# A gated attention and expert kernel: input rounding moved into the first steps, output projection one step later

## The chip, the cores and the metric

The kernel runs on one core of one Trainium2 chip. A core has five engines, each with its own queue of instructions: TensorE (PE in the profile), VectorE (DVE), ScalarE (ACT), GpSimd (POOL) and SyncE (SP, which here only issues transfers). They wait for each other by semaphores. The metric is the time of one execution on the device in microseconds, and the median over several runs.

## What is computed

```python
x = x + tanh(g_xattn) * xattn(layernorm(x), ctx)      # 4 batches of 256 tokens, 256 channels
x = x + tanh(g_ffn) * moe(layernorm(x))               # 64 experts, 6 for each token, 64 slots each
# xattn: h = ln(layernorm(x)); 8 groups of 2 heads, 128 channels a head
q, k, v = (fp8(bf16(clip(h / s_in))) * s_in @ W.T * w_scale for self attention)
qx      = the same with its own scale and weights; kx, vx = ctx @ w_kv_x.T   # cross attention
q, k, qx, kx = ln(each head)
out = concat(softmax(q k' / sqrt(128)) v, softmax(qx kx' / sqrt(128)) vx)    # 4096 channels
out = fp8(bf16(clip(out / smooth))) @ wproj.T * scale
```

`fp8(...)` is a rounding to 8-bit floats (4 exponent, 3 mantissa bits). All the rest is in 32 bits: matrix products take each operand as a high and a low part where it isn't exact.

## The kernel before

**Prologue (0 to some 60 us).** SP loads x by batch, then small vectors, the context, weights and eight scalars. DVE normalises each batch twice (`ln_step`), TensorE transposes (`transpose_h`), ScalarE applies the weights (`ln_out`) and divides by the four input scales (`quant_y`, eight activations a batch). `quant(b)` on DVE clips and rounds with four linked operations (clip, mask of the exponent, scale of the mask, addition), and `quant_sub(b)` on GpSimd subtracts into `xq`, the rounded rows. All four batches are done there, with two sets of scratch memory for them (`q_y`, `q_mg`). Key and value weights are transposed and split (`fill_kv`, `kv_hi`, `kv_lo`), then query weights.

**Attention loop.** There are 32 sub-heads: a = (group pair j, batch b, group in the pair). Step i of 34 (`NSUB + MAXLAG`) works on three of them: `s0 = sub(i)` is projected (`project_q`), normalised (`squares_q` on ACT, `sums` on DVE, `rstd_q` on GpSimd, `scaled_q` on DVE) and transposed (`fill_Tq`, `fill_Tk`; the high and low parts by `q_hi` and `qk_lo`); `s1 = sub(i-1)` has its four rows of `scores`, `maxes`, `exps`, `recip`, `p_norm` (GpSimd), transposes of the probabilities (`fill_pT`, `evac_pT`) and products with the values (`fill_pv`); `s2 = sub(i-2)` is rounded (`y_of`, `magic`, `round_cat`) and goes through the output projection `fill_op`, whose sum `add_acc` adds to `acc`. One half of the keys and values of a later batch is projected in every step (`project_kv`). Each engine's list is written out by hand in the order of execution.

**Buffers.** `proj_ps` holds one projection at a time. Two banks `aux_ps` alternate over all fills in the order that `all_fills` lists, so each fill waits until the one two places ahead is evacuated. `weight_fills(i, slot)` says which new weights are transposed in which step, by position `i % 8`.

**End.** In steps 32 and 33 `x1_stats(b)` adds the attention's result to x and takes the statistics for batch b, `f_pow(b)` (GpSimd) and `x1_norm(b)` (DVE) normalise, `fill_fT` transposes and `router_logits` scores the experts. Then the experts are chosen, rows gathered and 32 pairs of experts computed.

The profile's line numbers of the main parts: 509 `quant_sub`, 526 `rstd_of`, 541 `p_norm`, 548 and 551 `round_cat`, 665 `quant_y`, 792 `exps`, 806 `y_of`, 978 `weight_scales`, 987 to 990 `quant`, 1014 `kv_lo`, 1083 `scaled_q`, 1097 `maxes`, 1117 `magic`, 1143 to 1153 `x1_stats`, 1457 `project_q`, 1471 `fill_Tq`, 1501 `scores`, 1534 `fill_op`.

## Time and profile before

| | us |
|---|---|
| median of 3 runs (lowest, highest) | 824.04 (821.97, 824.12) |
| the profiled execution | 820.62 |
| its span, from the first to the last instruction | 818.80 |
| TensorE busy in the span | 724.2 (88%) |
| VectorE busy | 607.0 (74%) |
| ScalarE busy | 464.3 (57%) |
| GpSimd busy | 455.8 (56%) |

The span has some 60 us of prologue, about 570 of attention steps, 50 of tail and router, and 137 of experts. Busy shares say how full an engine is, not which one sets the pace: that is read from the waits in each stage. A duration in a timeline is that of a group of like instructions, and the time in square brackets is how long the engine stood idle before it and what ended this.

### The profile page before, as it was taken

Reading aid. Unit: us, or ns where it says so; the run is one execution under the profiler, and the core shown is the slowest. Engines: PE = TensorE matmul, PEld = TensorE weight load, DVE = VectorE, ACT = ScalarE, POOL = GpSimd, SP = SyncE. Lnnn points to the kernel's source line nnn. Section 1 sums busy time; section 2 is a strip of 40 time slices with the busy share of each in tenths; the row PEclk is TensorE's granted clock in tenths of the full one; section 3 lists DMA queues with packets and bytes.
Section 4 is the critical chain, followed back from the end, with each engine's and each line's share of the span. In section 5 each row is a group of like instructions: output and inputs, shape, how many; then the busy total and the mean of one; then the engine's idle time right before and its main releaser. Section 6 shows DMA issues by size and latency. Waiting matters only on the chain.

```text
span 818.8 us, 15329 instructions
## 1 busy us (share of the span) xinstructions
PE 724.2 (88%) x4859; PEld 586.4 (72%) x4859; DVE 607.0 (74%) x1290; ACT 464.3 (57%) x1178; POOL 455.8 (56%) x592
## 2 busy tenths in 40 slices
PE   3548999899999989999998999999976786999996
PEld 2536877788878777887877887887754554777775
DVE  6856888787888878888887888887887692444554
ACT  3646767667676766767666776766743231222221
POOL 3464767666667756676765667676655313222220
PEclk9869999999999999999999999999999796999999
DMA  5310000100000010000001010000020103666661
GB/s 181 107 54 26 1 27 1 49 30 27 27 1 27 1 53 26 26 27 2 27 1 52 2 33 27 1 2 0 1 59 1 38 28 109 192 186 189 198 193 53
DMA packets 44479, 42.74 MB, mean 52 GB/s; under 512 B 3718, under 2 KB 43387, under 8 KB 44411
## 3 DMA queue, kind: packets, MB, share of 16 engines
q1 hardware_dynamic: 42874, 36.62, 14.8%
q0 software_dynamic: 1536, 5.28, 2.4%
q8 instruction: 35, 0.57, 0.3%
q14 instruction: 34, 0.27, 0.1%
HBM read 39.52 MB, written 2.37 MB: 51 GB/s over the span
## 4 chain that ended last, share of the span: by engine, by line
PE 50%; DVE 19%; ACT 12%; issue 9%; POOL 7%; SPq 2%; DMA 1%; DVEq 0%; ACTq 0%; POOLq 0%
PE out_ps L1717 8%; PE aux_ps L1534 8%; PE proj_ps L1442 5%; ACT p_sb L792 5%; DVE q_tok L1083 4%; PE aux_ps L1471 4%; PE pT_ps L1510 4%; PE proj_ps L1433 4%; PE work_ps L1709 3%; POOL y_bf L548 3%; POOL catq L551 3%; PE work_ps L1731 2%; PE s_ps L1501 2%; ACT y_bf L806 2%; PE proj_ps L1457 2%
## 5 line engine op out<-in xcount | busy, mean ns | idle before, releaser
L541 POOL TENSOR_SCALAR p_sb<-p_sb,psum_row 128x256 f32<-128x256 f32 x256 | 121.1, 488 | 78.9 <-DVE psum_row L1102 78.8
L792 ACT ACTIVATE p_sb<-s_ps,negmax 128x256 f32<-128x256 f32 x256 | 118.0, 474 | 33.5 <-DVE negmax L1097 32.7
L1108 DVE COPY pT_sb<-pT_ps 128x512 f32<-128x512 f32 x128 | 87.7, 686 | 52.0 <-PE pT_ps L1510 50.9
L1520 PE MATMUL aux_ps<-pT_sb,v_sb 128*128 128x512 f32 x256 | 121.2, 595 | 3.5 <-DVE pT_sb L1108 3.5
L548 POOL TENSOR_TENSOR y_bf<-y_bf,mg_bf 128x512 bf16<-128x512 bf16 x64 | 86.1, 1345 | 63.8 <-DVE mg_bf L1120 63.8
L1501 PE MATMUL s_ps<-kT,qT 128*128 128x256 f32 x768 | 115.1, 292 | 6.0 <-DVE qT L1093 3.8
L1501 PEld LDWEIGHTS s_ps<-kT,qT 128*128 128x128 f32 x768 | 97.8, 190 | 15.9 <-issue 15.9
L526 POOL TENSOR_TENSOR rstd<-var,minus_half 128x8 f32<-128x8 f32 (+1 forms) x64 | 86.6, 1352 | 5.5 <-POOL var L522 0.4
L1097 DVE TENSOR_REDUCE negmax<-s_ps 128x2 f32<-128x512 f32 x128 | 86.2, 680 | 4.1 <-PE s_ps L1501 4.1
L1534 PE MATMUL aux_ps<-wpT,catq 128*128 128x256 f32 x512 | 70.9, 293 | 17.7 <-POOL catq L551 15.0
L806 ACT ACTIVATE y_bf<-aux_ps,rvec 128x256 bf16<-128x256 f32 x128 | 53.9, 478 | 51.0 <-PE aux_ps L1520 51.0
L551 POOL TENSOR_TENSOR catq<-y_bf,mg_bf 128x512 fp32r<-128x512 bf16 x64 | 79.7, 1245 | 5.0
L1534 PEld LDWEIGHTS aux_ps<-wpT,catq 128*128 128x128 f32 x512 | 65.4, 197 | 22.3 <-issue 16.9
L1717 PE MATMUL out_ps<-eo,onehot 128*128 128x256 f32 x512 | 73.3, 295 | 0.6 <-ACT eo L903 0.6
L1457 PE MATMUL proj_ps<-wqT,xq 128*128 128x256 f32 x512 | 67.8, 286 | 5.5 <-DVE k_tok L1072 5.5
L1510 PE MATMUL pT_ps<-ident,p_sb 128*128 128x128 f32 x512 | 71.9, 273 | 0.6 <-POOL p_sb L541 0.5
L1717 PEld LDWEIGHTS out_ps<-eo,onehot 128*128 128x128 f32 x512 | 65.3, 191 | 9.9 <-issue 8.6
L632 POOL DMA_INDIRECT gx<-rows_dram,idx_cur x32 | 33.0, 1030 | 68.2 <-DVE w_slot L1304 58.8
L1520 PEld LDWEIGHTS aux_ps<-pT_sb,v_sb 128*128 128x128 f32 x256 | 44.4, 191 | 35.2 <-issue 35.2
L1457 PEld LDWEIGHTS proj_ps<-wqT,xq 128*128 128x128 f32 x512 | 64.3, 193 | 5.7 <-DVE wqT L1025 5.7
L1063 DVE TENSOR_REDUCE ss<-sq 128x8 f32<-128x1024 f32 (+1 forms) x64 | 60.5, 945 | 9.3 <-ACT sq L727 5.0
L1510 PEld LDWEIGHTS pT_ps<-ident,p_sb 128*128 128x128 f32 x512 | 59.4, 140 | 5.9 <-POOL p_sb L541 1.8
(174 smaller groups left out, 1366.6 us busy)
## 6 DMA issues: line engine op xcount, KB each, us to landing
w_up_a<-in_L_ffn_gate_up_proj SPq DMA_DIRECT2D x16, 384.0 KB, 3.6
w_up_b<-in_L_ffn_gate_up_proj SPq DMA_DIRECT2D x16, 384.0 KB, 3.6
wp_raw<-in_L_xattn_wproj SPq DMA_DIRECT2D x16, 256.0 KB, 2.9
w_down_a<-in_L_ffn_down_proj SPq DMA_DIRECT2D x16, 192.0 KB, 3.6
w_down_b<-in_L_ffn_down_proj SPq DMA_DIRECT2D x16, 192.0 KB, 3.6
w_raw<-in_L_xattn_w_kv_x SPq DMA_DIRECT2D x8, 256.0 KB, 3.9
w_raw<-in_L_xattn_wq SPq DMA_DIRECT2D x7, 256.0 KB, 2.7
w_raw<-in_L_xattn_wqx SPq DMA_DIRECT2D x7, 256.0 KB, 3.0
```

Of the source, the lines that this page charges most:

```text
L526: nc.gpsimd.tensor_tensor(rstd[:, at], var8[:, at], minus_half[:, 0:w], ALU.pow).then_inc(rstd_ready, 1)
L541: ins = nc.gpsimd.tensor_scalar(p_sb[:, r, st, :], p_sb[:, r, st, :], rsum[:, r, st:st + 1], 1.0, ALU.mult, ALU.mult)
L548: nc.gpsimd.tensor_tensor(yc_bf[:, ty, :], yc_bf[:, ty, :], mg_bf[:, ty, :], ALU.add).then_inc(catq_ready, 1)
L551: nc.gpsimd.tensor_tensor(catq[:, s.gi, ty * HPG:(ty + 1) * HPG, :].rearrange("p a b -> p (a b)"), yc_bf[:, ty, :], mg_bf[:, ty, :], ALU.s ...
L792: ins = nc.scalar.activation(p_sb[:, r, st, :], s_ps[:, r % 2, st, :], ACT.Exp, bias=negmax[:, r, st:st + 1], accum_out=psum_row[:, r, st: ...
L1108: nc.vector.tensor_copy(pT_sb[:, r // 2, r % 2, :, :], pT_ps[:, r % 2, :, :]).then_inc(pT_ready, 1)
L1457: ins = nc.tensor.matmul(proj_ps[:, t, x * 256:(x + 1) * 256], xq[:, s.b, 3 * x, c, t * P:(t + 1) * P], wqT[:, s.gi, part, c, x * 256:(x + ...
L1501: ins = nc.tensor.matmul(s_ps[:, k % 2, st, :], qT[:, a, ty, h, st * P:(st + 1) * P], kT[:, b, ty, s.gi, :], start=(i == 0), stop=(i == 2))
L1510: ins = nc.tensor.transpose(pT_ps[:, r % 2, tt, st * P:(st + 1) * P], p_sb[:, r, st, tt * P:(tt + 1) * P], ident[:, :])
L1520: ins = nc.tensor.matmul(aux_ps[:, f.bank, :], v_sb[:, (2 * s.n + tt) % VRING, ty, s.gi, :], pT_sb[:, ty, :, tt, :], start=(tt == 0), stop ...
L1534: ins = nc.tensor.matmul(aux_ps[:, f.bank, tt * H:(tt + 1) * H], catq[:, s.gi, blk, tt * P:(tt + 1) * P], wpT[:, s.gi, part, blk, :], star ...
L1717: ins = nc.tensor.matmul(out_ps[:, n, :], onehot[:, u % 2, n * P:(n + 1) * P], eo[:, part, :], start=False, stop=False, skip_group_check=True)
```

## The change

Part one, rounding: batch 0 is rounded in two halves (keys and values first, whose subtraction DVE does itself), batch 1 in step 0, batch 2 in step 1 and batch 3 in step 3. ScalarE's `quant_y` of the latter two stands behind `exps(s1, 3)`. The scratch of batches 1 to 3 is now memory of the expert weights, whose first loads (`load_pair`) move behind the rounding. The keys of the second token tile of batch 0 are projected in the prologue, into `pT_ps`, with statistics of their own (`kv_ps`, `kv_stats`); in step 1 the key projection comes behind the first scores. The eight scalars are loaded from ScalarE's queue.

Part two, output: `fill_op` and `add_acc` work on `sub(i-3)`, stand ahead of `scores(s1, 3)` and `maxes(s1, 3)`, and the last one follows the loop. The WP fills of a first group go from position 1 to 2 of eight. `x1_stats` of batches 0, 1 and 2 stand at the ends of steps 28, 30 and 32, their `f_pow` and `x1_norm` and the router's first products move too.

The diff, cut to its core:

```diff
+
+        q_y0 = as_bf16(wp_raw[:, :, :, :].rearrange("p a b c -> p (a b c)"))
+        q_mg0 = as_bf16(qk_f[:, :, :].rearrange("p a b -> p (a b)"))
+        q_y1 = as_bf16(w_down_a[:, :, :, :].rearrange("p a b c -> p (a b c)"))
+        q_mg1 = as_bf16(w_up_a[:, :, :, :, :].rearrange("p u e c j -> p (u e c j)")[:, 0:4 * H])
...
-            if j < G // 2 and at in (0, 1, 3) and slot < 3:
-                return [{0: ("WQ", slot - 1, 2 * j + 1), 1: ("WP", slot - 1, 2 * j), 3: ("WP", slot - 1, 2 * j + 1)}[at]]
+            if j < G // 2 and at in (0, 2, 3) and slot < 3:
+                return [{0: ("WQ", slot - 1, 2 * j + 1), 2: ("WP", slot - 1, 2 * j), 3: ("WP", slot - 1, 2 * j + 1)}[at]]
...
-                names += [("O", s2.a)] if s2 else []
+                names += [("O", i - 3)] if i >= 3 else []
...
+            names += [("O", NSUB - 1)]
...
+
+        X_TYPES = (1, 2, 0, 3)
+
+        def kv_ps(n, t):
+            return pT_ps[:, :, :, :].rearrange("p a b c -> p a (b c)") if (n, t) == (0, 1) else proj_ps[:, :, :]
+
+        def kv_stats(n, t):
+            return slice(4, 8) if (n, t) == (0, 1) else slice(0, 4)
...
-            for i, name in enumerate(SCALARS):
-                sp.dma_start(scal[:, i:i + 1], t[name].partition_broadcast(P)).then_inc(scal_loaded, 16)
...
-            sp.wait_ge(xq_ready, NB - 1)
+            sp.wait_ge(xq_ready, 1)
...
+                if j == 0:
+                    sp.wait_ge(xq_ready, 2 * NB - 1)
+                    for u in range(2):
+                        load_pair(u, u)
...
-            def quant_sub(b):
-
-                pool.wait_ge(z_ready, b + 1)
-                nc.gpsimd.tensor_tensor(xq[:, b, :, :, :].rearrange("p a c k -> p (a c) k"), q_y[b % 2], q_mg[b % 2],
+            def quant_sub(b, half):
+
+                pool.wait_ge(z_ready, 2 * b + half)
+                part = slice(4 * half, 4 * half + 4)
+                y, mg = ((q_y1 if b else q_y0)[:, part, :], (q_mg1 if b else q_mg0)[:, part, :])
+                nc.gpsimd.tensor_tensor(xq[:, b, 2 * half:2 * half + 2, :, :].rearrange("p a c k -> p (a c) k"), y, mg,
                                         ALU.subtract).then_inc(xq_ready, 1)
 
...
-            quant_sub(0)
...
-
-            def rstd_of(seq, last, w):
...
+            quant_sub(0, 1)
...
             rstd_kv(0, 0)
-            quant_sub(1)
+            rstd_kv(0, 1)
...
-                if kv:
+                if kv and i > 1:
                     rstd_kv(*kv)
-                if i == 0:
-                    quant_sub(2)
...
+                if i == 1:
+                    rstd_kv(*kv)
...
                 if i == 0:
-                    quant_sub(3)
+                    quant_sub(1, 0)
+                    quant_sub(1, 1)
                 if s1:
                     p_norm(s1, 2)
                     p_norm(s1, 3)
+                if i in (1, 3):
+                    quant_sub(2 + i // 2, 0)
+                    quant_sub(2 + i // 2, 1)
+                if i == NSUB - 3:
+                    f_pow(0)
+                if i == NSUB - 1:
+                    f_pow(1)
                 if i == NSUB:
-                    f_pow(0)
-                    f_pow(1)
-
+
+                    pool.wait_ge(qk_normed, 2 * NSUB)
                     nc.gpsimd.memset(xs[:, :, H + E:], -1.0).then_inc(fillers_ready, 1)
...
-                wait(act, xq_ready, b - 1)
-                for ty in range(4):
+                wait(act, xq_ready, 2 * b - 1 if b > 1 else 0)
+                for t, ty in enumerate(X_TYPES):
                     for c in range(HC):
-                        ins = nc.scalar.activation(q_y[b % 2][:, ty * HC + c, :], yT[:, b, c, :], ACT.Copy,
+                        ins = nc.scalar.activation((q_y1 if b else q_y0)[:, t * HC + c, :], yT[:, b, c, :], ACT.Copy,
                                                    scale=rvec[:, INS + 2 * ty + c:INS + 2 * ty + c + 1])
+                    if t == 1:
+                        ins.then_inc(y_ready, 1)
                 ins.then_inc(y_ready, 1)
...
+            for i, name in enumerate(SCALARS):
+                act.dma_start(scal[:, i:i + 1], t[name].partition_broadcast(P)).then_inc(scal_loaded, 16)
...
             squares_kv(0, 0)
+            evac_v(0, 0)
+            squares_kv(0, 1)
+            evac_v(0, 1)
             wq_hi(0, 0)
             wq_hi(1, 0)
-            evac_v(0, 0)
             ln_out(2)
             ln_out(3)
-            quant_y(2)
...
                 weights_hi(i, 1)
-                if kv:
+                if kv and i > 1:
                     evac_v(*kv)
-                if i == 0:
-                    quant_y(3)
                 if s1:
                     q_hi(s1, 1)
...
+                if i == 1:
+                    squares_kv(*kv)
+                    evac_v(*kv)
...
                     exps(s1, 3)
+                if i in (1, 3):
+                    quant_y(2 + i // 2)
+                if s1:
                     y_of(s1, 0)
                 if s0:
                     evac_Tq(s0, 0)
                     q_hi(s0, 0)
                 if i == NSUB:
                     evac_fT(0)
-                if i == NSUB + 1:
                     evac_fT(1)
                     evac_fT(2)
...
-            def quant(b):
-
-                y, mg = q_y[b % 2], q_mg[b % 2]
-                dve.wait_ge(y_ready, b + 1)
-                wait(dve, xq_ready, b - 1)
+            def quant(b, half):
+
+                part = slice(4 * half, 4 * half + 4)
+                y, mg = ((q_y1 if b else q_y0)[:, part, :], (q_mg1 if b else q_mg0)[:, part, :])
+                dve.wait_ge(y_ready, 2 * b + half + 1)
+                if b == 1:
+                    dve.wait_ge(aux_filled, Fill("WQ", 1, 0).filled)
+                wait(dve, xq_ready, 2 * b - 1 if b > 1 else 0)
                 link(nc.vector.tensor_scalar(y, y, FP8_MAX, -FP8_MAX, ALU.min, ALU.max))
                 link(nc.vector.tensor_scalar(mg.bitcast(U16), y.bitcast(U16), 0x7F80, None, ALU.bitwise_and))
                 link(nc.vector.tensor_scalar(mg, mg, 2.0 ** -6, 24.0, ALU.max, ALU.mult))
-                nc.vector.tensor_tensor(y, y, mg, ALU.add).then_inc(z_ready, 1)
+                if (b, half) == (0, 0):
+                    link(nc.vector.tensor_tensor(y, y, mg, ALU.add))
+                    nc.vector.tensor_tensor(xq[:, 0, 0:2, :, :].rearrange("p a c k -> p (a c) k"), y, mg, ALU.subtract
+                                            ).then_inc(xq_kv_ready, 1)
+                else:
+                    nc.vector.tensor_tensor(y, y, mg, ALU.add).then_inc(z_ready, 1)
...
+            quant(0, 0)
             weight_scales()
-            quant(0)
             ctx_lo(0)
-            for i, (c, x) in enumerate(KV_ORDER):
+            ctx_lo(1)
+            for c, x in KV_ORDER:
                 kv_lo(c, x, 0)
-                if i == 1:
-                    ctx_lo(1)
             ctx_lo(2)
             ctx_lo(3)
+            quant(0, 1)
             for step in LN_STEPS[12:]:
                 ln_step(*step)
 
...
-            sums(0, 4)
-            quant(1)
+            sums(kv_seq(0, 0), 4)
+            sums(kv_seq(0, 1), 4)
             scaled_kv(0, 0)
             wq_lo(0, 0)
             wq_lo(1, 0)
+            scaled_kv(0, 1)
...
                 if i == NSUB + 1:
-                    x1_norm(1)
-                if i == NSUB:
-
-                    dve.wait_ge(gate_ready, 1)
-                    link(nc.vector.tensor_scalar(gate[:, 1:2], gate[:, 0:1], scal[:, 4:5], scal[:, 5:6],
-                                                 ALU.mult, ALU.mult))
-                    wait_sum(0)
-                    x1_stats(0)
-                if kv:
+                    x1_norm(2)
+                if kv and i > 1:
                     sums(kv_seq(*kv), 4)
-                if i == 0:
-                    quant(2)
...
-                if kv:
+                if kv and i > 1:
                     scaled_kv(*kv)
                 if s1:
                     recip(s1, 1)
+                if i == 1:
+                    sums(kv_seq(*kv), 4)
+                    scaled_kv(*kv)
                 if s2:
                     magic(s2, 1)
                 if i == NSUB:
-                    wait_sum(1)
-                    x1_stats(1)
-                if i == NSUB + 1:
-                    x1_norm(2)
+                    x1_norm(0)
+                    x1_norm(1)
...
                 if i == 0:
-                    quant(3)
+                    quant(1, 0)
                 if s1:
                     evac_pT(s1, 1)
                 weights_lo(i, 3)
+                if i >= 3:
+                    add_acc(sub(i - 3))
                 if s1:
                     maxes(s1, 3)
-                if s0 and s0.gi == 0:
-                    qk_lo(s0.n, "TKs")
-                if s2:
-                    add_acc(s2)
-                if s1:
                     recip(s1, 2)
                 if s0:
                     scaled_q(s0)
+                if i == 0:
+                    quant(1, 1)
+                if i in (1, 3):
+                    quant(2 + i // 2, 0)
                 if s1:
                     recip(s1, 3)
+                if s0 and s0.gi == 0:
+                    qk_lo(s0.n, "TKs")
+                if s1:
                     evac_pT(s1, 2)
+                if i in (1, 3):
+                    quant(2 + i // 2, 1)
+                if s1:
                     magic(s1, 0)
                 if s0:
                     qk_lo(s0.a, "TQ")
...
-                if i == NSUB:
-                    wait_sum(2)
-                    x1_stats(2)
-                    x1_norm(0)
+                if i == NSUB - 4:
+
+                    dve.wait_ge(gate_ready, 1)
+                    link(nc.vector.tensor_scalar(gate[:, 1:2], gate[:, 0:1], scal[:, 4:5], scal[:, 5:6],
+                                                 ALU.mult, ALU.mult))
+                if i in (NSUB - 4, NSUB - 2, NSUB):
+                    wait_sum((i - NSUB + 4) // 2)
+                    x1_stats((i - NSUB + 4) // 2)
+            f = Fill("O", NSUB - 2)
+            dve.wait_ge(aux_free[f.bank], f.drained)
+            add_acc(sub(NSUB - 1))
...
-                if j == 0:
-                    pe.wait_ge(xq_ready, b + 1)
-                wait(pe, qk_normed, seq)
-                wait(pe, v_ready, 2 * n + t)
+                if n == 0:
+                    pe.wait_ge(xq_kv_ready, 1)
+                elif j == 0:
+                    pe.wait_ge(xq_ready, 2 * b + 1)
+                if seq == kv_seq(0, 1):
+                    pe.wait_ge(ctx_ready, 4)
+                else:
+                    wait(pe, qk_normed, seq)
+                    wait(pe, v_ready, 2 * n + t)
...
-                wait(pe, qk_normed, seq)
-                wait(pe, v_ready, min(s.a + 2, 2 * NU))
+                if s.j == 0:
+                    pe.wait_ge(xq_ready, 2 * s.b + 1)
+                wait(pe, qk_normed, seq if s.a else kv_seq(0, 0) + 1)
+                wait(pe, v_ready, min(s.a + 2, 2 * NU) if s.a else 1)
...
             project_kv(0, 0)
+            project_kv(0, 1)
+            fill_wq(0, 0)
+            fill_wq(1, 0)
             transpose_h(2)
             transpose_h(3)
-            fill_wq(0, 0)
-            fill_wq(1, 0)
             for i in range(NSUB + MAXLAG):
                 s0, s1, s2, kv = sub(i), sub(i - 1), sub(i - 2), kv_at(i)
-                if kv:
+                if kv and i > 1:
                     project_kv(*kv)
...
+                if i == 1:
+                    project_kv(*kv)
...
+                if i >= 3:
+                    fill_op(sub(i - 3))
                 if s1:
                     scores(s1, 3)
-                if i == NSUB + 1:
-                    fill_fT(1)
-                    fill_fT(2)
-                    router_logits(0)
-                if s2:
-                    fill_op(s2)
...
                 if i == NSUB:
                     fill_fT(0)
+                    fill_fT(1)
+                    fill_fT(2)
+                    router_logits(0)
+                    router_logits(1)
                 if i == NSUB + 1:
-                    router_logits(1)
                     fill_fT(3)
-                    router_logits(2)
+            fill_op(sub(NSUB - 1))
+            router_logits(2)
```

## Rows read from the trace of the kernel before

**Rows 1.** Busy time by stage: window, length, busy us and count by engine, granted clock, DMA share, GB/s
```profile
232.92:375.05 142.13, 135.75 (x920) 113.24 (x921) 116.86 (x227) 99.60 (x251) 96.35 (x128) 1.00 0.08 23
...
601.82:637.03 35.21, 23.23 (x122) 16.12 (x123) 27.39 (x63) 12.41 (x35) 19.89 (x26) 0.92 0.13 34
```

**Rows 2.** Waits of TensorE, eight steps from 216.33 to 358.46: us in total, times, longest
```profile
PE aux_ps L1534 <- POOL catq L551: 2.4, 5, 0.7
PE aux_ps L1471 <- DVE q_tok L1083: 2.1, 8, 0.3
...
PE aux_ps L1534 <- DVE wkvT L1014: 0.9, 1, 0.9
```

**Rows 3.** Timeline of odd step 13: start, duration, instruction, idle time before and releaser
```profile
279.13 0.77 PEld L1501 LDWEIGHTS s_ps<-kT,qT 128*128 128x128 f32 x6 [0.84 <-issue]
...
284.33 2.14 PE L1534 MATMUL aux_ps<-wpT,catq 128*128 128x256 f32 x16 [0.75 <-POOL catq L551]
...
284.80 1.65 POOL L526 TENSOR_TENSOR rstd<-var,minus_half 128x8 f32<-128x8 f32 x1
...
287.19 1.20 DVE L1083 TENSOR_TENSOR q_tok<-proj_ps,rstd 128x1024 f32<-128x1024 f32 x1
...
288.45 0.66 PE L1471 MATMUL aux_ps<-ident,q_tok 128*128 128x128 f32 x4 [0.26 <-DVE q_tok L1083]
```

**Rows 4.** Timeline of step 14, the output projection behind new key weights
```profile
305.24 2.17 PE L1534 MATMUL aux_ps<-wpT,catq 128*128 128x256 f32 x16 [0.88 <-DVE wkvT L1014]
```

**Rows 5.** Timeline of the prologue and the first steps
```profile
18.90 0.62 DVE L978 TENSOR_SCALAR wscale<-vec,scal 128x2 f32<-128x2 f32 x4 [2.74 <-DMA scal<-in_g_ffn]
...
48.39 3.75 PE L1457 MATMUL proj_ps<-wqT,xq 128*128 128x256 f32 x16 [5.50 <-DVE k_tok L1072]
...
66.02 1.67 PE L1501 MATMUL s_ps<-kT,qT 128*128 128x256 f32 x12
...
70.42 2.13 PE L1457 MATMUL proj_ps<-wqT,xq 128*128 128x256 f32 x16
...
78.31 0.66 PE L1471 MATMUL aux_ps<-ident,q_tok 128*128 128x128 f32 x4 [0.75 <-DVE q_tok L1083]
...
82.39 1.68 PE L1501 MATMUL s_ps<-kT,qT 128*128 128x256 f32 x12
```

**Rows 6.** Timeline of the rounding of batch 2 on ScalarE, VectorE and GpSimd
```profile
38.91 3.32 ACT L665 ACTIVATE wp_raw<-acc,rvec 128x256 bf16<-128x256 f32 x8
...
43.35 0.68 DVE L987 TENSOR_SCALAR wp_raw<-wp_raw 128x2048 bf16<-128x2048 bf16 x1
...
45.52 1.23 DVE L990 TENSOR_TENSOR wp_raw<-wp_raw,qk_f 128x2048 bf16<-128x2048 bf16 x1
...
46.83 4.07 POOL L509 TENSOR_TENSOR xq<-wp_raw,qk_f 128x2048 fp32r<-128x2048 bf16 x1 [1.21 <-DVE wp_raw L990]
```

**Rows 7.** Timeline of the tail, VectorE's mask operation alone and beside GpSimd
```profile
627.21 0.29 DVE L1117 TENSOR_SCALAR mg_bf<-y_bf 128x512 uint16<-128x512 uint16 x1
...
632.56 1.29 POOL L551 TENSOR_TENSOR catq<-y_bf,mg_bf 128x512 fp32r<-128x512 bf16 x1
...
632.87 1.13 DVE L1117 TENSOR_SCALAR mg_bf<-y_bf 128x512 uint16<-128x512 uint16 x1
```

**Rows 8.** Timeline of the tail: last scores, residuals, last output projection
```profile
609.32 1.67 PE L1501 MATMUL s_ps<-kT,qT 128*128 128x256 f32 x12 [1.08 <-issue]
...
610.04 1.79 DVE L1143 SCALAR_TENSOR_TENSOR x_sb<-acc,gate,x_sb 128x256 f32<-128x256 f32 x2
...
613.01 1.28 DVE L1097 TENSOR_REDUCE negmax<-s_ps 128x2 f32<-128x512 f32 x2
...
628.35 0.87 DVE L1143 SCALAR_TENSOR_TENSOR x_sb<-acc,gate,x_sb 128x256 f32<-128x256 f32 x2
...
630.32 0.17 DVE L1153 TENSOR_SCALAR f_mv<-f_mv 128x2 f32<-128x2 f32 x1
...
637.03 3.75 PE L1534 MATMUL aux_ps<-wpT,catq 128*128 128x256 f32 x16 [2.84 <-POOL catq L551]
```

58 lines of the change are left out of this document (25 added, 33 removed).

## The prediction, made before the changed kernel ran

> **What bounds the kernel now.** I read the windows by stage first. In each of three equal stretches of eight steps TensorE is busy 135.7 of 142.1 us [rows 1]: the attention loop runs at TensorE's pace, and what it can win there is 6.4 us in eight steps. In the last two steps (601.8 to 637.0) TensorE has 23 us of work in 35 and DVE 27: there a chain through DVE decides. The waits of TensorE name the 6.4 us: five waits of the output projection for `catq` (2.4 us), eight waits of the query transposes for `q_tok` (2.1), one for the aux bank held by the key weights (0.9), and small ones [rows 2]. The timeline of one odd step shows the order [rows 3]: the projection starts at 284.33 after 0.75 us, and DVE's `scaled_q` at 287.19 then releases the transposes at 288.45 after 0.26. The prologue is chains: two waits (2.74 and 5.50 us) and a first score at 66.02 [rows 5].
>
> **Output projection one step later.** The wait for `catq` goes, since sub-head `i-3` was rounded a step ago. What is late next is `scaled_q`. New order from 282.6 of [rows 3] on: projection 2.0, scores 0.95, values 1.9 on TensorE; `add_acc`, maximum, reciprocal on DVE; then `scaled_q`, which cannot start before `rstd` ends (284.80 + 1.65 = 286.45). It would run at 286.5 instead of 287.19, so the step wins 0.7, not 0.75 + 0.26. With 0.35 us waits (even steps) the same count gives 0.4. In the step that fills new key weights the projection stands right behind them and still waits for the bank until 305.24 [rows 4]; the scores that stood ahead now come behind, and `scaled_q` ends 0.9 later: a loss, three times. Steps 7 and 8 of eight have no such wait and win nothing. Moving the WP fills from an odd step (with 0.75 and 0.84 us idle [rows 3]) to an even one costs some 0.4 per eight. Step by step from 4 to 31 this sums to **-5.2 us** (bounds: 0, if the fills eat it; -13, if every wait of [rows 2] in 28 steps went). Step 2 has no projection any more, and the last one runs in the idle end: **-1.1** by `rstd`'s chain (bounds 0 and -2.4).
>
> **Start.** (a) Scale loads move to ScalarE's queue; DVE's 2.74 us wait for them [rows 5] goes, but half of batch 0's rounding now stands in that place: three operations at half of 0.68, an addition at half of 1.23, a subtraction between 0.62 (bfloat16 out) and 1.2 (as `scaled_q`, as many fp32 out) [rows 3, 6]. I take 1.0: about 2.9 us in all, so the weights' high halves start where they did, and their low halves, with no rounding of 3.4 us ahead, some 2.4 earlier. (b) The second half of it and the last layer norm follow on DVE; the last scaling there meets GpSimd's `quant_sub(0,1)`, half of 4.07 [rows 6], and may wait it out (below): the first `sums` comes 1.1 later than now. (c) The second key tile has PSUM of its own, so no second round of squares, rstd and `k_tok` stands before the first query projection: it starts at 40.9 instead of 48.39. (d) From there squares, sums, half a rounding, `scaled_q`, the second half, transposes and `qk_lo` take 14.6 (17.6 now): first scores at **55.5 against 66.02**. (e) In step 1 the key projection moves behind these scores, and the next query projection waits for its `scaled_kv`: 8.2 instead of 4.4 us later, 63.7 against 70.42. Sum of the start: **-6.7**.
>
> **Rounding in steps 1 and 3.** ScalarE needs 3.3 us a batch (eight activations), DVE 0.68, 0.69, 0.69, 1.23, GpSimd 4.07 [rows 6]; halves cost about half. Before, most of it lay beside chains that waited anyway. Now it stands between `scaled_q` and `qk_lo(TQ)`, which releases the next scores. Now scores follow 4.1 us after the transposes (82.39, which the timeline gives for step 2, less 78.31 [rows 5]). New, counted from the transposes: `quant_y` follows the last exponentials and gives its first half at +0.6, DVE rounds until 2.5, evacuates until 3.3, rounds until 5.2, then `magic` (1.0) and `qk_lo` (0.7): 6.9, 2.8 us more than now, with nothing hidden since TensorE waits in order.
>
> **The lock.** [rows 7] show more: `mg_bf` L1117 takes 0.29 us alone and 1.13 us from 632.87, beside GpSimd's `catq` (632.56 to 633.85): it ends 0.15 after it. DVE's chain gave way between two linked operations, and waited GpSimd's whole operation. In the new steps GpSimd's `quant_sub` of the first half (2.1 us, from 4.07 [rows 6]) becomes ready while DVE rounds the second half, and that of the second half while DVE runs `magic`: twice 2.1 us. So 11.1 in place of 4.1: **+7.0** a batch, and +0.7 for `rstd_kv`, which queues on GpSimd behind `quant_sub` and the late `round_cat`. Two batches: **+15.4** (bounds: 2 x 2.8 = 5.6 without the lock; 2 x 11, if all of the rounding, 3.3 + 3.7 + 4.1, is exposed).
>
> The Trainium skill ("SBUF — State Buffer", section "SBUF: two separate sides") has the rule for this: DVE and GpSimd share a port pair, held for a whole instruction, by whichever starts first. The trace agrees (1.13 against 0.29 us). By that rule each of the collisions counted above costs up to 2.1 us; without it the change would be a gain (rival 1).
>
> **Residuals moved forward.** `x1_stats` costs 2.1 us undisturbed (628.35 to 630.49) and about 3 beside GpSimd (610.04 to 613.01) [rows 8]. In step 32 two of them hold the chain. At the ends of steps 28 and 30 they stand ahead of the maxima and of `qk_lo(TX)`, for which TensorE already idles 0.84 us in an odd step [rows 3]: 2.1 each, with the gate's 0.3: **+4.5**. In exchange the tail from the last scores (609.32) to the last projection (637.03), 27.7 us, loses two `x1_stats`, but gains two norms before the third maximum, two router products ahead of the last `fill_pT`, and `round_cat` queues behind `f_pow(2)`: I count 25.7, **-2.0** (bounds +1 and -5.5, the two `x1_stats` in full). The final product starts after an idle engine as now (3.75 us).
>
> **At nothing.** The expert weights `load_pair` move on SP's queue behind a wait for the last rounding (step 3); behind it stand query weights due in step 6, 35 us later, and their own use is after 676 us. The eight scale loads issue on an engine that has nothing to do before 11 us. If they slowed the rows of x by a queue's turn, it would be some 0.4 us (one issue, the timeline's 0.43 each). The f_stat tiles only move. WQ fills and PSUM banks keep their order.
>
> **Sum.** -6.7 + 15.4 - 5.2 - 1.1 + 2.5 = **+4.9** on the profiled execution (820.62 us for a span of 818.8). The median of the runs shown is 824.04, 3.4 above it, so I add the sum to the median: **829.0**. About 0.3% (2.5 us) is what a measurement of this kernel tells from no change.
>
> **Rivals.**
> 1. *No lock where I count it (faster).* For it: no row before shows a two-input DVE operation beside the long `quant_sub`, only beside `y_bf` and `catq`. Against: same engine, same form as `catq`. Then 8.4 less in steps 1 and 3 and 3 less in the start (b and d): 829 - 11.4 = 817.6. It turns to a gain from the point where GpSimd holds DVE up for less than 0.4 of its time.
> 2. *TensorE's waits all go (faster).* -13 instead of -5.2: 821.2. For it: 2.4 and 2.1 us stand in [rows 2]; against: `rstd` ends at 286.45 whatever the projection does.
> 3. *Nothing on balance.* One of the two deferred batches, or one of the two GpSimd collisions in each, is hidden: 4 to 5 us less, 824.5.
> 4. *All of the rounding exposed (slower).* 22 instead of 15.4: 835.6. For it: each engine hands to the next; against: halves overlap.
>
> **Chances.** Forecast 0.43 (826.6 to 832), rival 1 0.24, rival 2 0.10, rival 3 0.14, rival 4 0.09. Faster 0.34, same 0.14, slower 0.52. The range leaves out the ends of rivals 1 and 4: 815 to 836; slower alone would be 826.6 to 836.
>
> **What would show it.** Right: first scores near 55 us; in steps 1 and 3 a gap of about 7 us on TensorE before the scores, with DVE rounding operations of 0.35 us stretched to above 2 beside `quant_sub`; no wait of the projection for `catq` except the last; the wait for `q_tok` still there; TensorE idle some 2 us in steps 29 and 31. Wrong: unstretched rounding operations (rival 1); eight steps in 138 us or less (rival 2); the first scores later than 60 or before 52 us, where my hand-made chain of the start would be off by more than the rest of the sum.

## The result, and the profile after

The changed kernel takes 835.41 us (median of 4 runs, 834.18 to 836.05), the kernel before, run beside it, 824.08 (821.97 to 824.33): a ratio of 1.0137 (95% interval 1.0116 to 1.0159). It is slower, as forecast, by 11.3 us where 4.9 were forecast. The profiled executions differ by more, 833.0 against 818.8 us of span, because the profiled one of the kernel before lies in the lower part of what that kernel does from run to run (820.62 us, where all its runs of this study took 819.5 to 825.4). The differences read from the two traces so add up to 3 us more than those of the medians; in which stretch the 3 us lie is not shown.

Where it went is read from one mark: the start of each step's query projection (L1457 before, L1503 after). The table gives, for each stretch, the forecast and the difference of the two profiled executions in us (rounded, so that the rows add up to 0.1 more than the sum).

| stretch | forecast | measured |
|---|---|---|
| up to the query projection of step 1 | -6.7 | -2.4 |
| step 1 (rounding of batch 2) | +7.7 | +10.6 |
| step 2 | -1.1 | -0.7 |
| step 3 (rounding of batch 3) | +7.7 | +8.2 |
| steps 4 to 30, with two `x1_stats` | -0.7 | -2.5 |
| from step 31 to the end | -2.0 | +1.1 |
| sum | +4.9 | +14.2 |

**The gap and what stands behind it.** TensorE's timeline of the changed kernel, from the transposes of step 1 to the query projection of step 2 (answering to the last two lines of [rows 5]):

```profile
77.08 0.66 PE L1517 MATMUL aux_ps<-ident,q_tok 128*128 128x128 f32 x4 [0.74 <-DVE q_tok L1115]
...
87.59 2.90 PE L1547 MATMUL s_ps<-kT,qT 128*128 128x256 f32 x12 [5.05 <-issue]
90.29 3.25 PE L1566 MATMUL aux_ps<-pT_sb,v_sb 128*128 128x512 f32 x4
...
94.54 2.05 PE L1503 MATMUL proj_ps<-wqT,xq 128*128 128x256 f32 x16
```

From the transposes to the scores it is 10.5 us (forecast 11.1, before 4.1). But the scores then take 2.90 us, and took 1.68 before [rows 5]; the products with the values take 3.25, and 1.88 before. From the start of the scores to the query projection of step 2 it is 7.0 us; before it was 4.0 (82.39 to 86.34). The windows of this stretch show why (start and end, length, busy us and count of PE, PEld, DVE, ACT and POOL, granted clock, DMA share, GB/s):

```profile
82.50:87.60 5.10, 0.05 (x2) 0.04 (x1) 5.00 (x7) 0.01 (x1) 3.46 (x3) 0.87 0.00 0
87.60:90.30 2.70, 2.70 (x13) 2.70 (x14) 2.14 (x4) 2.58 (x5) 2.45 (x4) 0.50 0.00 0
90.30:93.40 3.10, 3.10 (x6) 1.24 (x6) 2.25 (x6) 1.72 (x8) 1.76 (x4) 0.56 0.01 3
93.40:96.00 2.60, 2.60 (x24) 2.60 (x23) 1.48 (x5) 1.33 (x3) 1.42 (x3) 1.00 0.28 83
```

TensorE stands still for 5 us, and is then granted 0.50 of its clock (1.2 GHz of 2.4) until about 93 us; behind the gap of step 3 (5.49 us, until 130.73) the scores take 2.90 us as well. DVE is busy for 5.00 of the 5.10 us of the gap; its timeline and GpSimd's show with what:

```profile
80.93 2.29 POOL L522 TENSOR_TENSOR xq<-w_down_a,w_up_a 128x1024 fp32r<-128x1024 bf16 x1
...
81.27 2.22 DVE L1015 TENSOR_SCALAR w_up_a<-w_up_a 128x1024 bf16<-128x1024 bf16 x1
...
84.30 2.12 POOL L522 TENSOR_TENSOR xq<-w_down_a,w_up_a 128x1024 fp32r<-128x1024 bf16 x1 [1.09 <-DVE w_down_a L1021]
84.46 2.10 DVE L1149 TENSOR_SCALAR mg_bf<-y_bf 128x512 uint16<-128x512 uint16 x1
```

L1015 takes 0.43 us in the first half, where GpSimd is idle; L1149 takes 0.29 elsewhere. Both are stretched until GpSimd's `quant_sub` ends (0.27 and 0.14 us behind its end), as [rows 7] let one expect.

**The start.** Timeline lines answering to the rest of [rows 5]:

```profile
5.15 0.75 DVE L981 BATCH_NORM_STATS2 q_tok<-x_sb 128x6 f32<-128x256 f32 x2 [5.15 <-DMA x_sb<-in_x]
...
40.51 3.75 PE L1419 MATMUL aux_ps<-center,w_raw 128*128 128x128 f32 x16 [3.05 <-DVE wqT L1056]
43.92 2.75 PE L1503 MATMUL proj_ps<-wqT,xq 128*128 128x256 f32 x16
...
58.52 2.90 PE L1547 MATMUL s_ps<-kT,qT 128*128 128x256 f32 x12 [2.71 <-issue]
...
68.06 2.87 PE L1503 MATMUL proj_ps<-wqT,xq 128*128 128x256 f32 x16 [3.13 <-DVE k_tok L1104]
```

The first rows of x are waited for until 5.15 us (3.75 before); the query weights take 3.75 us for 16 products; and the first scores take 2.90, where the kernel before had 1.67 [rows 5]. In the kernel before the query weights took 1.95 us:

```profile
40.94 1.95 PE L1380 MATMUL aux_ps<-center,w_raw 128*128 128x128 f32 x16
```

The first scores wait for a stretched operation here too: `qk_lo` (L1125, 0.68 us alone) takes 2.61 beside `quant_sub` of batch 1.

```profile
55.36 2.50 POOL L522 TENSOR_TENSOR xq<-w_down_a,w_up_a 128x1024 fp32r<-128x1024 bf16 x1 [2.02 <-DVE w_down_a L1021]
...
55.80 2.61 DVE L1125 TENSOR_TENSOR qT<-qk_f,qT 128x512 fp32r<-128x512 f32 x1
```

**The steady steps.** The window of eight steps that answers to the first of [rows 1], and TensorE's waits in it, answering to [rows 2]:

```profile
226.60:366.92 140.32, 134.69 (x923) 112.75 (x922) 117.58 (x227) 99.91 (x251) 97.37 (x129) 1.00 0.08 24
```

```profile
PE aux_ps L1517 <- DVE q_tok L1115: 3.0, 8, 0.6
PE aux_ps L1580 <- DVE wkvT L1045: 1.6, 1, 1.6
```

Eight steps take 140.32 us and not 142.13. The waits of the output projection for `catq` (2.4 us) are gone; those for `q_tok` grew from 2.1 to 3.0 and the one behind new key weights from 0.9 to 1.6, as forecast.

**Residuals and tail.** DVE's line of the first residual (`x1_stats(0)`, at the end of step 28) and the maxima behind it:

```profile
570.79 0.89 DVE L1175 SCALAR_TENSOR_TENSOR x_sb<-acc,gate,x_sb 128x256 f32<-128x256 f32 x2
...
573.45 1.28 DVE L1129 TENSOR_REDUCE negmax<-s_ps 128x2 f32<-128x512 f32 x2
```

TensorE's timeline, the scores that waited for this, and then the tail:

```profile
575.43 0.95 PE L1547 MATMUL s_ps<-kT,qT 128*128 128x256 f32 x6 [2.42 <-DVE qT L1125]
...
621.75 1.67 PE L1547 MATMUL s_ps<-kT,qT 128*128 128x256 f32 x12 [1.09 <-issue]
...
632.36 3.65 PE L1566 MATMUL aux_ps<-pT_sb,v_sb 128*128 128x512 f32 x4 [2.13 <-DVE pT_sb L1140]
...
636.64 1.19 PE L1617 MATMUL proj_ps<-ident,xs 128*128 128x128 f32 x8
637.98 2.00 PE L1626 MATMUL proj_ps<-gateT,hxT 128*128 128x64 f32 x16 [0.16 <-ACT hxT L842]
639.82 0.61 PE L1556 MATMUL pT_ps<-ident,p_sb 128*128 128x128 f32 x4
...
649.98 3.42 PE L1580 MATMUL aux_ps<-wpT,catq 128*128 128x256 f32 x16 [2.75 <-POOL catq L563]
```

From the last first-scores (621.75) to the last projection (649.98) it is 28.2 us; before it was 27.7 [rows 8], and 25.7 were forecast. The router's transposes and products (636.64 to 639.98) stand ahead of the last transposes of probabilities.

### The profile page after: what moved, and what is told of

Read it like the earlier page. It is cut to its first block, busy times and chain, and to the rows that moved or that the text cites. A ratio compares the mean times of both kernels' runs of the same rounds, so it can differ in the third digit from the quotient of the medians.

```text
span 833.0 us, 15352 instructions
## 1 busy us (share of the span) xinstructions
PE 728.9 (88%) x4859; PEld 591.0 (71%) x4859; DVE 625.4 (75%) x1307; ACT 466.3 (56%) x1178; POOL 456.3 (55%) x595
## 3 DMA queue, kind: packets, MB, share of 16 engines
q1 hardware_dynamic: 41722, 36.61, 14.2%
## 4 chain that ended last, share of the span: by engine, by line
PE 59%; DVE 23%; issue 8%; ACT 5%; POOL 4%; DMA 1%; POOLq 0%; DVEq 0%; ACTq 0%
PE out_ps L1766 8%; PE s_ps L1547 6%; PE proj_ps L1503 6%; PE pT_ps L1556 5%; PE proj_ps L1486 5%; PE aux_ps L1566 5%; DVE q_tok L1115 4%; PE aux_ps L1580 4%; PE aux_ps L1517 4%; PE work_ps L1758 3%; PE proj_ps L1477 3%; POOL rstd L538 3%; DVE pT_sb L1140 3%; DVE ss L1095 2%; PE work_ps L1780 2%
## 5 line engine op out<-in xcount | busy, mean ns | idle before, releaser
L553 POOL TENSOR_SCALAR p_sb<-p_sb,psum_row 128x256 f32<-128x256 f32 x256 | 125.2, 504 | 80.2 <-DVE psum_row L1134 78.8
L1547 PE MATMUL s_ps<-kT,qT 128*128 128x256 f32 x768 | 116.2, 295 | 20.0 <-issue 15.2
L1566 PE MATMUL aux_ps<-pT_sb,v_sb 128*128 128x512 f32 x256 | 124.1, 608 | 5.6 <-DVE pT_sb L1140 5.6
L1547 PEld LDWEIGHTS s_ps<-kT,qT 128*128 128x128 f32 x768 | 101.3, 196 | 30.8 <-issue 30.7
L1503 PE MATMUL proj_ps<-wqT,xq 128*128 128x256 f32 x512 | 67.4, 285 | 3.1 <-DVE k_tok L1104 3.1
L776 ACT ACTIVATE qk_f<-aux_ps,vec 128x512 f32<-128x512 f32 x64 | 49.8, 778 | 32.7 <-PE aux_ps L1517 17.1
L1503 PEld LDWEIGHTS proj_ps<-wqT,xq 128*128 128x128 f32 x512 | 64.1, 192 | 3.3 <-issue 3.3
```

What stands on the lines that cost most here:

```text
L553: ins = nc.gpsimd.tensor_scalar(p_sb[:, r, st, :], p_sb[:, r, st, :], rsum[:, r, st:st + 1], 1.0, ALU.mult, ALU.mult)
L1503: ins = nc.tensor.matmul(proj_ps[:, t, x * 256:(x + 1) * 256], xq[:, s.b, 2 + x, c, t * P:(t + 1) * P], wqT[:, s.gi, part, c, x * 256:(x + ...
L1547: ins = nc.tensor.matmul(s_ps[:, k % 2, st, :], qT[:, a, ty, h, st * P:(st + 1) * P], kT[:, b, ty, s.gi, :], start=(i == 0), stop=(i == 2))
L1566: ins = nc.tensor.matmul(aux_ps[:, f.bank, :], v_sb[:, (2 * s.n + tt) % VRING, ty, s.gi, :], pT_sb[:, ty, :, tt, :], start=(tt == 0), stop ...
```

## Experiments

Each kernel was timed against the kernel before on the same chip. The table shows the result, and the same mark as above: how much later than in the kernel before the query projection of a step starts in the profiled execution, and the end of the span (us).

| kernel | us | ratio to before (95%) | step 1 | 2 | 4 | 28 | 31 | end |
|---|---|---|---|---|---|---|---|---|
| changed | 835.41 | 1.0137 (1.0116 to 1.0159) | -2.4 | 8.2 | 15.6 | 10.2 | 13.1 | 14.2 |
| o_later | 810.62 | 0.9872 (0.9848 to 0.9896) | -1.1 | -0.2 | -1.3 | -6.6 | -8.5 | -10.7 |
| res_back | 827.67 | 1.0065 (1.0045 to 1.0085) | -2.5 | 5.9 | 14.6 | 9.2 | 7.3 | 7.6 |
| warm | 835.18 | 1.0165 (1.0141 to 1.0189) | -2.5 | 7.1 | 14.8 | 9.4 | 13.8 | 14.4 |
| scal_sp | 833.26 | 1.0142 (1.0119 to 1.0166) | -3.8 | 6.8 | 14.3 | 8.9 | 11.8 | 13.0 |
| warm18 | 831.08 | 1.0098 (1.0064 to 1.0132) | -2.5 | 5.2 | 12.3 | 7.0 | 9.9 | 11.1 |
| pool_wait | 837.60 | 1.0166 (1.0124 to 1.0208) | -3.6 | 5.6 | 14.8 | 11.1 | 15.5 | 16.5 |
| tail_fix | 834.69 | 1.0145 (1.0113 to 1.0178) | -2.8 | 7.8 | 15.2 | 9.8 | 12.7 | 13.7 |
| dve_sub | 830.36 | 1.0089 (1.0058 to 1.0120) | -3.2 | 5.1 | 11.4 | 5.9 | 8.8 | 9.9 |
| no_round | 817.02 | 0.9930 (0.9909 to 0.9950) | -2.6 | -0.6 | -1.7 | -7.0 | -4.1 | -2.8 |
| tail_router | 830.94 | 1.0102 (1.0081 to 1.0123) | -3.3 | 7.3 | 14.7 | 9.3 | 12.2 | 9.8 |
| mended | 820.18 | 0.9967 (0.9951 to 0.9982) | -3.0 | 3.6 | 9.5 | 4.3 | 2.4 | 0.7 |
| o_warm | 807.82 | 0.9824 (0.9800 to 0.9849) | -2.8 | -1.9 | -3.0 | -8.3 | -10.2 | -12.2 |

The kernel before had medians of 822.1 to 824.1 us beside the four groups of runs, and the changed kernel stands in the group with 824.1. Differences between two rows are therefore taken from the ratios (0.001 is 0.82 us), which tell them to some 2 to 4 us; below that the marks and lines of the traces decide. Of each kernel there is one trace, and kernels that have the same code in a stretch show how far one execution differs from another there. Over steps 1 to 3 the changed kernel, res_back, scal_sp, tail_fix and tail_router, alike in code, lost 17.1 to 18.1 us against the kernel before. From step 31 on res_back and mended, alike in code, stand at +0.3 and -1.7.

### o_later: the later projection alone, on the kernel before

```diff
-            if j < G // 2 and at in (0, 1, 3) and slot < 3:
+            if j < G // 2 and at in (0, 2, 3) and slot < 3:
...
+                if i >= 3:
+                    fill_op(sub(i - 3))
                 if s1:
                     scores(s1, 3)
...
-                if s2:
-                    fill_op(s2)
...
+            fill_op(sub(NSUB - 1))
```

The cut shows TensorE's list; `add_acc` moves with it on VectorE.

> The kernel before with one part of the change: the output projection and its sum one step later, ahead of scores row 3, the WP fills at position 2, the last projection behind the loop; rounding and residuals as before. Theory A (the wait for catq goes and scaled_q's rstd limits what is won): the changed kernel's steps 4 to 27 stand 5.4 us closer to the kernel before than at step 4, and step 2 wins 0.7, so some 7 to 7.5 us in all: 816.5 to 817.5 us beside 824.1. Rival (the steady gain only exists because the rounding in steps 1 and 3 left slack behind): within 2 us of 824.

11.5 us faster than the kernel before by the medians and 10.5 by the ratio, more than theory A said; the rival fell. Between steps 4 and 31 it wins 7.2 us, in the same steps as the changed kernel does, so the gain does not hang on the rounding. From step 31 on it wins 2.2 more: from the last first-scores to the last projection it is 26.9 us (27.7 before), and the last projection takes 2.15 us, at full clock, and 3.75 before [rows 8]. That clock can be chance: behind the same wait of 0.51 us the last projection takes 3.65 us in res_back and 2.14 in mended. The 1.1 us won ahead of step 1 stand where the edit changes nothing.

### res_back: the residuals back in steps 32 and 33

```diff
-                if i in (NSUB - 4, NSUB - 2, NSUB):
-                    wait_sum((i - NSUB + 4) // 2)
-                    x1_stats((i - NSUB + 4) // 2)
+                if i == NSUB:
+                    wait_sum(2)
+                    x1_stats(2)
+                    x1_norm(0)
```

> The changed kernel with the residuals (x1_stats, f_pow, x1_norm, the router's first products) back in steps 32 and 33 as in the kernel before. Theory A (moving them costs 2.5 us at the ends of steps 28 and 30 each, and gives nothing back in the tail): some 5 us faster than the changed kernel, 830 to 831. Theory B (the prediction's sum: 4.5 lost, 2.0 won in the tail): 2.5 us faster, 833. Rival: the tail is shorter by the move as meant, and taking it back costs: 836 or more.

5.9 us faster than the changed kernel by the ratios (7.7 by the medians): theory A, whose 5 us lie within what the ratios tell; theory B's 2.5 and the rival do not. Steps 28 and 30 no longer lose (they win 0.6 each where the changed kernel lost 1.8), 4.8 us together, about the 4.5 of the forecast. From the last first-scores to the last projection it is 26.9 us and not 28.2, though two `x1_stats` came back into this stretch. So the tail of the changed kernel had to hold something dearer.

### warm and warm18: products that keep TensorE busy in the gaps

```diff
+                if i in (2, 4):
+                    pe.wait_ge(exp_done, s1.m - 1)
+                    for r in range(18):
+                        nc.tensor.matmul(s_ps[:, 0, 0, 0:P], ident[:, :], ident[:, :], start=True, stop=True)
                 if s1:
                     scores(s1, 0)
```

> The changed kernel with 32 more products of the identity with itself on TensorE ahead of the first scores of steps 2 and 4, into a score bank that these scores overwrite: TensorE works through most of the 5.1 and 5.5 us gaps. Theory clock (TensorE's granted clock is 0.5 for some 5.7 and 3 us behind those gaps because it stood still in them, and this costs 2.6 and 1.8 us beyond the gaps): the scores behind them take 1.7 us and not 2.90, granted clock 1.0, and the run is some 4 us faster, 831 to 832. Rival (the clock falls there for another reason, or the time is lost on DVE anyway): 835.4 or slower, since the added products can only delay.

> The changed kernel with 18 added products of the identity ahead of the first scores of steps 2 and 4 (each takes two instructions of 0.114 us, 4.1 us in all, so that they end before qT is ready; with 32 they took 7.31 us and held the scores up by 1.9). Theory clock: the granted clock stays 1.0 behind the gaps, the scores there take 1.7 us and not 2.90, and steps 1 and 3 are 2.6 and 1.5 us shorter: about 4 us, 831 to 832. Rival (what the clock gives back is lost again on GpSimd, whose rstd and p_norm set when the next projection starts): 834 to 835.4.

The edit shown is that of warm18; warm has 32 in place of 18. With 32 the products took 7.31 us and held the scores up to 89.00 (12.4 us behind the transposes and not 10.5); the scores took 1.68 us, but what the clock gave back was spent: 835.18 us, nothing won, as the rival had it. With 18, TensorE's timeline of warm18:

```profile
81.95 4.18 PE L1648 MATMUL s_ps<-ident 128*128 128x128 f32 x36
...
87.17 1.66 PE L1547 MATMUL s_ps<-kT,qT 128*128 128x256 f32 x12 [1.04 <-issue]
88.67 1.88 PE L1566 MATMUL aux_ps<-pT_sb,v_sb 128*128 128x512 f32 x4
...
91.55 2.12 PE L1503 MATMUL proj_ps<-wqT,xq 128*128 128x256 f32 x16
```

The scores start 10.5 us behind the transposes, as they did, take 1.66 us and not 2.90, the values 1.88 and not 3.25, and the next projection starts 4.4 us behind the scores and not 7.0 (in step 3 4.7 and not 5.4). Steps 1 to 3 lose 14.7 us where the five kernels without these products lose 17.1 to 18.1; the run is 3.2 us faster by the ratios, 4.3 by the medians. So the lost clock is on the path; the rival (given back on GpSimd) fell.

### pool_wait and dve_sub: the lock, taken away in two ways

```diff
                 if i in (1, 3):
+                    pool.wait_ge(qk_lo_ready["TQ"], s0.a + 1)
                     quant_sub(2 + i // 2, 0)
```

> The changed kernel with GpSimd's two quant_sub of steps 1 and 3 held back until VectorE has written the low part of qT, so that they no longer run beside VectorE's rounding and magic. Theory lock: L1015 takes 0.43 us and not 2.22, the mask L1149 0.29 and not 2.10, the scores of steps 2 and 4 come 3.6 us sooner; GpSimd's later norms give some of it back: 2 to 5 us faster than the changed kernel, 830.5 to 833.5. Rival (no lock, the operations were long for another reason): both operations stay above 2 us, and the later subtraction makes the run slower, 837 to 839.

```diff
+                if b > 1:
+                    link(nc.vector.tensor_tensor(y, y, mg, ALU.add))
+                    nc.vector.tensor_tensor(xq[:, b, 2 * half:2 * half + 2, :, :].rearrange("p a c k -> p (a c) k"),
+                                            y, mg, ALU.subtract).then_inc(xq_ready, 1)
...
-                    quant_sub(2 + i // 2, 0)
-                    quant_sub(2 + i // 2, 1)
```

> The changed kernel with the subtraction of batches 2 and 3 on VectorE (1.23 us a half) and none on GpSimd. Theory lock: 3.6 us of stretched operations go and 2.46 us of subtraction come, in each of steps 1 and 3: 2 to 3 us faster, 832.5 to 833.5. Rival (no lock): VectorE's chain is 2.46 us longer in each step, 840.

The timeline of pool_wait, VectorE, GpSimd and TensorE:

```profile
80.04 0.43 DVE L1016 TENSOR_SCALAR w_up_a<-w_up_a 128x1024 bf16<-128x1024 bf16 x1
...
81.43 0.29 DVE L1150 TENSOR_SCALAR mg_bf<-y_bf 128x512 uint16<-128x512 uint16 x1
...
82.73 4.23 POOL L522 TENSOR_TENSOR xq<-w_down_a,w_up_a 128x1024 fp32r<-128x1024 bf16 x2 [3.01 <-DVE qT L1126]
...
82.75 1.66 PE L1548 MATMUL s_ps<-kT,qT 128*128 128x256 f32 x12 [1.44 <-issue]
...
83.76 0.68 DVE L1130 TENSOR_REDUCE negmax<-s_ps 128x2 f32<-128x512 f32 x1
...
85.55 1.96 DVE L1126 TENSOR_TENSOR qT<-qk_f,qT 128x512 fp32r<-128x512 f32 x1
...
90.13 1.02 POOL L538 TENSOR_TENSOR rstd<-var,minus_half 128x4 f32<-128x4 f32 x1
...
91.97 3.62 PE L1504 MATMUL proj_ps<-wqT,xq 128*128 128x256 f32 x16 [3.41 <-issue]
```

In step 1 the operations behave as the lock (GpSimd's operation holding VectorE's up) says: both stretched ones are back at 0.43 and 0.29 us, the scores stand 6.9 us behind the transposes (75.84), TensorE's gap is 1.44 us, and the scores run at full clock. In step 3 the gap is 1.88 us and the scores take 2.90 us again. But the time is that of the rival: 837.6 us. GpSimd now subtracts from 82.73 to 86.96, the key norm `rstd` behind it and behind `round_cat` ends at 91.15, and the next query projection, which waits for the scaled keys, stands still for 3.41 us and then runs at half clock itself. The stall was moved, not removed: step 1 is 1.4 us shorter than in the changed kernel and step 2, with the slow projection, 1.6 longer; step 3 is as long, and step 4, which begins with such a projection too (3.00 us behind a wait of 3.40), is 1.7 longer. Over steps 1 to 4 it loses 19.4 us, where the changed kernel loses 17.4 and its four likes 16.5 to 17.5; the ratios alone would not tell that it is slower. In dve_sub GpSimd is out of the way; the timeline of its step 1:

```profile
82.88 1.22 DVE L1015 TENSOR_TENSOR xq<-w_down_a,w_up_a 128x1024 fp32r<-128x1024 bf16 x1
...
84.34 0.29 DVE L1150 TENSOR_SCALAR mg_bf<-y_bf 128x512 uint16<-128x512 uint16 x1
...
85.67 2.90 PE L1548 MATMUL s_ps<-kT,qT 128*128 128x256 f32 x12 [2.70 <-issue]
...
88.37 2.05 PE L1567 MATMUL aux_ps<-pT_sb,v_sb 128*128 128x512 f32 x4
```

The mask takes 0.29 us, TensorE's gap is 2.70 us and not 5.05, and the clock is back for the values, 2.05 us and not 3.25. Steps 1 and 3 are 2.3 and 1.1 us shorter, and the run is 4.0 us faster by the ratios (5.0 by the medians), more than the 2 to 3 expected: the chain alone was counted (the scores stand 9.4 us behind the transposes and not 10.5), not the clock behind the shorter gap (the next projection stands 5.7 us behind the scores and not 7.0). 0.9 of the 4.3 us at the end of the span stand in the start already, where the edit changes nothing. The rival without a lock, 840, fell.

The Trainium skill ("SBUF — State Buffer", section "SBUF: two separate sides") limits the lock to VectorE's operations with two inputs in SBUF or in a mode that takes both ports. The lines agree: beside GpSimd's 4.23 us the maxima, which read PSUM, keep their 0.68 us, and the subtraction of two SBUF operands takes 1.96 and not 0.68.

### no_round: what the rounding in steps 1 and 3 costs in all

```diff
-                if i in (1, 3):
-                    quant_y(2 + i // 2)
...
-                    quant(2 + i // 2, 0)
...
-                    quant(2 + i // 2, 1)
...
-                    quant_sub(2 + i // 2, 0)
-                    quant_sub(2 + i // 2, 1)
...
-                                             xq[:, b, ty, c, t * P:(t + 1) * P],
+                                             xq[:, min(b, 1), ty, c, t * P:(t + 1) * P],
```

> The changed kernel without the rounding of batches 2 and 3 (no quant_y, quant and quant_sub in steps 1 and 3; the projections of batches 2 and 3 read the rounded rows of batch 1, so these batches are not computed; all else is as it was). Theory A (rounding in steps 1 and 3 costs what the traces show there, 10.6 + 8.2 us, the clock lost behind its gaps with it): steps 1 and 3 as in the kernel before, 16.5 to 19 us faster than the changed kernel, 816.5 to 819. The prediction's sum: 15.4 faster, 820. Rival (much of the time in step 1 is the key projection behind the scores, which stays): 8 to 12 faster, 823.5 to 827.

The kernel leaves the rounding of batches 2 and 3 out; the query projection, not in the cut, reads the rows of batch 1 too. It is 17.0 us faster than the changed kernel by the ratios and 18.4 by the medians, theory A. What is left of the loss in steps 1 to 3 is 0.9 us (from -2.6 to -1.7; 2.0 lost in step 1, 1.1 won in steps 2 and 3), so the rounding costs some 17 us there: the key projection behind the scores is not what costs. Steps 28 and 30 still lose their 1.8 us each, so the residuals are a cost of their own.

### scal_sp: the scalars on SyncE's queue again

```diff
-            for i, name in enumerate(SCALARS):
-                act.dma_start(scal[:, i:i + 1], t[name].partition_broadcast(P)).then_inc(scal_loaded, 16)
...
+            for i, name in enumerate(SCALARS):
+                sp.dma_start(scal[:, i:i + 1], t[name].partition_broadcast(P)).then_inc(scal_loaded, 16)
```

> The changed kernel with the eight scalars loaded from SyncE's queue behind the first weights, as before. Theory A (their 1,024 small packets, started beside the first rows of x, hold these up from 3.75 to 5.15 us, and all of the start with them): the first statistics start at 3.75 again and the run is 1.4 us faster, 834.0. Rival (the late rows are chance, and the scales are then waited for as before): first statistics at 5.15, or 1 to 2 us lost again at weight_scales: 835.4 to 837.

The first statistics of x in the timeline of scal_sp:

```profile
3.47 0.75 DVE L981 BATCH_NORM_STATS2 q_tok<-x_sb 128x6 f32<-128x256 f32 x2 [3.47 <-DMA x_sb<-in_x]
```

3.47 us and not 5.15, and the first query projection starts 1.7 us sooner than in the changed kernel. The times do not tell 1.4 us (833.26; the ratio is that of the changed kernel), but the late rows are not chance: in all nine traces with the scalars on ScalarE's queue the first statistics start at 4.94 to 5.15 us, in all five with them on SyncE's at 3.47 to 3.75. The rival's second half, a wait at `weight_scales`, did not come: these run at 19.03 us and at 20.72 in the changed kernel. The Trainium skill ("DMA: Bandwidth & Descriptors", section "Issuing engines are not separate DMA queues") says that transfers of different issuing engines interleave on the same DMA engines, so that a second queue saves only issue time; these lines agree.

### tail_fix and tail_router: what holds the last projection

```diff
-                if i == NSUB + 1:
-                    x1_norm(2)
...
                 if s2:
                     magic(s2, 1)
+                if i == NSUB + 1:
+                    x1_norm(2)
```

> The changed kernel with x1_norm(2) of step 33 behind VectorE's last magic, as before, and not ahead of it. Theory order (that norm waits 0.83 us for f_pow and takes 2.47 us, and the last projection waits for the rounding behind it): the last projection starts 2.5 to 3.3 us sooner behind the last scores, 832 to 833. Rival (GpSimd's queue is what the last projection waits for, whatever VectorE does): within 0.5 us of 835.4.

```diff
                 if i == NSUB:
                     evac_fT(0)
+                if i == NSUB + 1:
                     evac_fT(1)
                     evac_fT(2)
...
                 if i == NSUB:
                     fill_fT(0)
+                if i == NSUB + 1:
                     fill_fT(1)
                     fill_fT(2)
                     router_logits(0)
                     router_logits(1)
-                if i == NSUB + 1:
                     fill_fT(3)
```

> The changed kernel with fill_fT(1), fill_fT(2) and the router's products of batches 0 and 1 at the end of step 33, behind the last transposes of probabilities, and not ahead of them at the end of step 32. Theory A (these 3.2 us of TensorE stand on the way to the last values and the last projection): from the last first-scores to the last projection 25 to 26.5 us and not 28.2; 833 to 834.5. Rival (VectorE and GpSimd set that chain, TensorE only fills in): 28.2 us and 835.4, or slower, since the products then come behind the last projection's wait.

tail_fix: 27.8 us from the last first-scores to the last projection, 0.4 less, and 834.69 us, no clear change; theory order fell. Its timeline shows what took the norm's place:

```profile
643.54 1.16 POOL L560 TENSOR_TENSOR y_bf<-y_bf,mg_bf 128x512 bf16<-128x512 bf16 x1
643.71 1.14 DVE L1146 TENSOR_SCALAR y_bf<-y_bf 128x512 bf16<-128x512 bf16 x1 [0.95 <-ACT y_bf L825]
644.78 1.15 POOL L563 TENSOR_TENSOR catq<-y_bf,mg_bf 128x512 fp32r<-128x512 bf16 x1
644.88 1.19 DVE L1149 TENSOR_SCALAR mg_bf<-y_bf 128x512 uint16<-128x512 uint16 x1
```

GpSimd's `round_cat` of the other half stands behind `f_pow(2)` and so runs just here; the two operations of `magic` (0.28 and 0.29 alone) give way to it. tail_router: 25.7 us from the last first-scores to the last projection and not 28.2. From step 31 to the end it wins 3.5 us on the changed kernel, the run 2.9 by the ratios (4.5 by the medians); theory A. TensorE's timeline:

```profile
620.84 1.67 PE L1548 MATMUL s_ps<-kT,qT 128*128 128x256 f32 x12 [1.08 <-issue]
...
631.48 3.59 PE L1567 MATMUL aux_ps<-pT_sb,v_sb 128*128 128x512 f32 x4 [2.14 <-DVE pT_sb L1141]
...
635.71 0.66 PE L1557 MATMUL pT_ps<-ident,p_sb 128*128 128x128 f32 x4
...
646.54 2.14 PE L1581 MATMUL aux_ps<-wpT,catq 128*128 128x256 f32 x16 [1.26 <-POOL catq L563]
```

The last transposes of probabilities come 4.2 us behind the start of the slow values and not 7.5, and the last projection runs at full clock, 2.14 us and not 3.42; TensorE waits 1.26 us ahead of it and not 2.75, since the router's products now lie there. In all seven kernels with the changed kernel's wait of 2.75 us, itself among them, the last projection took 3.38 to 3.75 us.

### mended and o_warm: what can be had

```diff
+                if i == 0:
+                    pe.wait_ge(ctx_ready, 4)
+                    for r in range(22):
+                        nc.tensor.matmul(pT_ps[:, 0, 0, 0:P], ident[:, :], ident[:, :], start=True, stop=True)
                 if s0:
                     project_q(s0)
```

mended joins the edits of res_back, scal_sp and dve_sub with 10 products a gap; o_warm is o_later with the edit shown, and 27 such products ahead of `fill_Tq(s0, 0)` of step 0.

> The changed kernel with four costs taken back at once: residuals where they were (as in res_back), scalars on SyncE's queue (as in scal_sp), subtraction of batches 2 and 3 on VectorE (as in dve_sub), and 10 added products of the identity in each of the two gaps, which are then 2.7 us long. Theory additive: 835.4 - 7.7 - 2.1 - 5.0 - 2 = some 818.5, so faster than before but not than the later projection alone (810.6): rounding inside the steps still costs 8 us. Rival (the costs overlap): 821 to 824.

> The later projection alone (the kernel of the run o_later, rounding and residuals as before) with 22 and 27 added products of the identity in TensorE's two waits of step 0, into a bank of the probabilities that nothing uses yet. Theory clock: the granted clock there, 0.5 from 48 to 64 us in the kernel before, stays 1.0; the first projection takes 2.1 us and not 3.75, the transposes, key products and scores behind it half, and the first steps come 3 to 4 us sooner: 806.5 to 808. Rival (chains of VectorE and GpSimd hold these steps, the clock is not on the way): 810 to 811.

mended: 820.18 us, between the additive 818.5 and the overlap's 821, so the four costs add up but for some 2 us, which is no more than the groups differ by. It is faster than before by 0.33% (0.18 to 0.49%), yet 9.6 us behind o_later. o_warm is the fastest of all kernels here: 2.8 us ahead of o_later by the medians, 1.6 by the mark of step 1 and 1.5 at the end of the span. Its timeline of the start:

```profile
49.49 2.13 PE L1461 MATMUL proj_ps<-wqT,xq 128*128 128x256 f32 x16
...
62.66 1.66 PE L1505 MATMUL s_ps<-kT,qT 128*128 128x256 f32 x12 [0.35 <-issue]
```

The first projection takes 2.13 us and not 3.75 [rows 5], though it starts 0.7 us later than in o_later (48.83), and the first scores stand at 62.66, where they stood at 65.19 in o_later and at 66.02 before.

## Why the prediction was right in sign and under half the size

**Right.** The mechanism of the loss: GpSimd's subtraction holds VectorE's rounding, and TensorE waits in order. 10.5 and 11.2 us from transposes to scores stand against 11.1 forecast; two operations in each of these steps were stretched to 2.1 to 2.2 us, in the places named. The two terms of it hold one by one: without the lock 6.9 us were forecast and came (step 1 of pool_wait), and the lock, counted at 4.2 us, took 3.6. Rival 1 (no lock) fell. The later projection wins what `rstd` leaves, not the full waits: `q_tok` is waited for longer, as said; `x1_stats` in steps 28 and 30 costs 4.8 us against 4.5 (res_back). The stretch of the start that was counted at 14.6 us, first query projection to first scores, took 14.6.

**Wrong.** The step that failed is one of size, not of kind: TensorE's work behind a gap was counted at full clock. Three terms of the sum were mis-sized, the first two of them for this reason in the main.

1. *Rounding, +15.4.* "6.9, 2.8 us more than now" and the 11.1 us end at the first score; everything behind it was counted at the durations of [rows 3] and [rows 5]. Behind the gaps that the prediction itself forecast, the granted clock was 0.5 for some 6 and 3 us; [rows 5] have such a case, a projection of 3.75 us behind a wait of 5.50. Steps 1 and 3 came out 18.8 us longer by the marks, some 17 of them by the rounding (no_round), and products in the gaps took 3.6 us off them (warm18). With these the way from the scores to the next projection is 0.4 and 0.8 us longer than before, about the +0.7 forecast for `rstd_kv`. Rival 4 (22) comes near that size, but for another reason: the chain to the first score was not longer than forecast. That its time, 835.6 us, is the one measured is luck, since the start and the tail missed too.
2. *Start, -6.7*, was -2.4. Of the missing 4.3 us, 1.4 are the rows of x: the eight scale loads stood "at nothing", or at 0.4 us if they slowed these rows, and cost 1.4 to 1.7 (scal_sp). 1.8 are the query weights (3.75 us for 1.95), which put the first query projection off, and 1.2 the first scores (2.90 for 1.67), both at half clock behind waits of 3.05 and 2.71 us; that sums to 4.4.
3. *Tail, -2.0.* The 25.7 us counted were 28.2, where they were 27.7 before. The count had the two router products ahead of the last `fill_pT`, but not that these transposes release a chain of 10 us. With the old order it is 26.9 (res_back, o_later), with the products behind the transposes 25.7 (tail_router); that this is the very number of the count is luck, since the count had them ahead. Of the 3.5 us that tail_router wins from step 31 on, 2.5 are the order; the rest stands behind the start of the last projection, which ran at full clock (2.14 us for 3.42).
4. In the other direction, the later projection was worth more: 7.2 us in steps 4 to 31 and not 5.2, and 10.5 in all by the ratio (o_later). Why the steps win more than counted was not looked into.

By the traces the misses of all stretches add up to 9.3 us (14.2 for 4.9); by the medians the forecast missed by 6.4. Two smaller slips: by rival 1's own numbers (11.4 us of lock in a sum of +4.9) the change turns to a gain once GpSimd holds VectorE up for less than some 0.57 of its time, not 0.4; and VectorE's share in the bound of 2 x 11 is 3.3 us by [rows 6], not 3.7.

By parts, from the ratios: the later projection -10.5 us, the rounding with its start +15.9 (res_back against o_later), the residuals +5.9 (the changed kernel against res_back); each is known to some 2 to 3 us.

## What to carry to other kernels

A forecast of a gap on TensorE is not finished where the gap ends: the work behind it has to be counted at the lower clock, and products that fill the gap, sized to end before the data come, took most of that cost away here (4.2 us of them in a gap of 5.1), and too many gave nothing (7.3 us of them). A transfer or a subtraction that is moved to a free queue still meets the others in the DMA engines and in the memory port; price the move by what runs beside it at the new place. A change of several parts is worth splitting: here the later projection alone wins 1.3%, and the rounding and the residuals that came with it lose more than that together.

## What the runs showed of the hardware

The loss of clock varies by itself: in two executions with the same code in step 1 (the changed kernel and res_back), the scores behind a gap of 5.05 and 5.06 us took 2.90 and 2.70 us and the values 3.25 and 2.45, and step 1 took 2.1 us less in the second (step 3 1.3 us more). The same holds in the tail: behind a wait of 0.51 us, in the same code, the last projection took 3.65 us in res_back and 2.14 in mended. A short wait can cost the clock too: behind 1.88 us (step 3 of pool_wait) the scores took 2.90 us, behind 1.44 (step 1) 1.66. The product of the identity with itself, 128 by 128 in 32 bits, takes two instructions of 0.114 us each at full clock.
